# A two-layer graph network: the second layer's frames move from between the layers into the first layer's loop

## What is computed

```
x = layernorm(x + L0(x, edge_index, edge_attr_4, edge_attr_32, ...))
x = layernorm(x + L1(x, edge_weight, edge_attr_3, edge_index, ...))
# L1, per edge:
R = relu(edge_weight[:, None] @ w1 + b1) @ w2 + b2
r = edge_attr_3 / norm(edge_attr_3)
msg = sum over paths of R * (spherical harmonics of r) * x[src] * Wigner 3j
out = out.at[dst].add(msg)
```

## Time and profile before

| | |
|---|---|
| median of 3 runs | 4217.16 us (4216.61 to 4221.31) |
| profiled execution | 4217.1 us, of which the span of its instructions is 4215.3 us |
| busy in the span | PE 3586.2, PEld 2173.2, DVE 3226.0, ACT 2200.7, POOL 3022.9 us |
| layer 0's gathers | first start 27.0, last start 2039.6 us |
| layer 1's gathers | first start 2101.7, last start 4144.9 us |
| granted TensorE clock | 0.934 of full speed in the mean |

### The profile page before, as it was taken

The page is one execution under the profiler, slowest core; times in us unless marked ns, Lnnn a source line. Parts: engine busy times, 40 slices in busy tenths (PEclk is TensorE's granted clock), DMA queues, the critical chain, the costliest instruction groups (busy, mean ns, idle before and its releaser), DMA issues.

```text
span 4215.3 us, 77958 instructions
## 1 busy us (share of the span) xinstructions
PE 3586.2 (85%) x24746; PEld 2173.2 (52%) x24746; DVE 3226.0 (77%) x4478; ACT 2200.7 (52%) x6571; POOL 3022.9 (72%) x3143
## 2 busy tenths in 40 slices
PE   5888888888888888888439999999999999999995
PEld 3555555555555555555315555555555555555553
DVE  6666666666666666666789988888888888888887
ACT  2555555555555555555315555555555555555553
POOL 5777777777777777777357777777777777777772
PEclk7998999999999999999769999999999999999998
DMA  3111111111111111111221221221212122221212
GB/s 101 30 25 30 25 30 30 25 30 25 30 25 30 30 25 30 25 30 25 37 89 39 46 46 37 47 44 39 47 37 47 37 46 44 40 47 37 47 37 32
DMA packets 214486, 159.83 MB, mean 38 GB/s; under 512 B 124769, under 2 KB 188002, under 8 KB 213474
## 3 DMA queue, kind: packets, MB, share of 16 engines
q0 software_dynamic: 100352, 51.58, 8.6%
q1 hardware_dynamic: 84946, 90.16, 8.2%
q10 hardware_dynamic: 29170, 17.88, 1.5%
HBM read 148.94 MB, written 10.43 MB: 38 GB/s over the span
## 4 chain that ended last, share of the span: by engine, by line
POOL 55%; issue 23%; PE 10%; DVE 7%; DMA 3%; DVEq 1%; POOLq 0%; ACT 0%; SPq 0%; ACTq 0%
POOL rows L352 55%; PE red L668 6%; PE wps L655 3%; DVE prod L972 2%; DMA rows<-x_rows,src 2%; DVE q L1024 1%; PE wps L648 1%; DMA src<-in_src 1%; DVE t_a L1010 0%; PE acc L682 0%; DVEq L1052 0%; POOLq L369 0%; DVE table L1048 0%; DVE t_b L896 0%; DVE work L877 0%
## 5 line engine op out<-in xcount | busy, mean ns | idle before, releaser
L352 POOL DMA_INDIRECT rows<-x_rows,src x1568 | 1507.3, 961 | 598.0 <-issue 560.4
L352 POOL DMA_INDIRECT rows<-in_x,src x1568 | 1514.7, 966 | 508.7 <-issue 498.8
L668 PE MATMUL red<-prod,ident 128*128 128x336 f32 (+2 forms) x6272 | 1753.7, 436 | 0.0
L668 PEld LDWEIGHTS red<-prod,ident 128*128 128x128 f32 x6272 | 1145.0, 192 | 647.5 <-issue 189.5
L476 ACT ACTIVATE gap<-iota,slot_plan 128x128 bf16<-128x128 f32 x3136 | 945.7, 387 | 91.9 <-DVE t_b L1075 81.9
L972 DVE TENSOR_TENSOR prod<-wps,q 128x896 f32<-128x896 f32 x784 | 836.6, 1084 | 192.4 <-PE wps L655 175.3
L648 PE MATMUL wps<-bias_parts,ones 64*128 64x448 bf16 (+1 forms) x2352 | 464.1, 391 | 558.9 <-DVE prod L966 330.8
L655 PE MATMUL wps<-w_sb,hidden 64*128 64x256 f32 (+1 forms) x4704 | 910.5, 490 | 0.0
L494 ACT ACTIVATE sums<-red 128x336 f32<-128x336 f32 (+2 forms) x392 | 168.4, 430 | 1074.7 <-PE red L668 1073.7
L648 PEld LDWEIGHTS wps<-bias_parts,ones 64*128 64x128 bf16 x2352 | 114.6, 94 | 1084.7 <-DVE prod L966 430.5
L1006 DVE TENSOR_TENSOR t_a<-rows,geo 128x384 f32<-128x384 f32 x98 | 55.2, 563 | 674.4 <-DMA rows<-in_x,src 674.4
(11 more groups left out here) (123 smaller groups left out, 2993.6 us busy)
## 6 DMA issues: line engine op xcount, KB each, us to landing
mlp<-in_dist SPq DMA_DIRECT2D x196, 256.0 KB
mlp<-in_feat SPq DMA_DIRECT2D x98, 256.0 KB
rows<-in_x,src POOLq DMA_INDIRECT x1568
rows<-x_rows,src POOLq DMA_INDIRECT x1568
frames<-prod ACTq DMA_DIRECT2D x4, 1764.0 KB, 5.8
geo<-frames ACTq DMA_DIRECT2D x98, 72.0 KB
src<-in_src SPq DMA_DIRECT2D x196, 8.0 KB, 1.6
geo<-in_sh ACTq DMA_DIRECT2D x98, 32.0 KB, 1.7
```

Source lines behind the costliest of these rows:

```text
L352: nc.gpsimd.indirect_dma_start(out=rows[z][:, t, :], out_offset=None, in_=table_rows, in_offset=bass.IndirectOffsetOnAxis(ap=src_sb[z][:, ...
L668: ins = nc.tensor.matmul(red[:, bank * 512:bank * 512 + cols], ident[:], pr[:, i, :, a:b, :], start=(i == 0), stop=(i == MUL - 1))
```

## The change

The frames are made two chunks at a time, at the end of body0 of each even chunk (49 times 17 instructions on 32 columns), in a buffer of their own, and ACT stores each piece to the same place in DRAM in the following body. The squares (now on ACT), their sums and the root move to the setup, before the node table. The reciprocal is taken per piece. Before layer 1 only ACT waits, for the count of all stores. ACT's copies of the frames to PSUM in layer 1 are as before, and so is the rest of both loops.

```diff
+        lengths = sb("lengths", [P, CHUNKS * TILES])
+        frame = sb("frame", [P, FRAME_TILES, GEO[1]])
+        frame_tmp = sb("frame_tmp", [P, 5, FRAME_TILES])
...
+            def square_lengths():
+                act.wait_ge(loaded["rel"], 16)
+                for square, ts in zip(squares, square_tiles):
+                    nc.scalar.activation(square, rel_sb[:, ts, :], ACT.Square).then_inc(rel_squared, 1)
+
+            def root_lengths():
+                act.wait_ge(lengths_squared, 2)
+                nc.scalar.activation(lengths[:], lengths[:], ACT.Sqrt).then_inc(lengths_ready, 1)
+
+            def store_frames(i, r):
+                act.wait_ge(frames_ready, r)
+                act.dma_start(frame_dram[:, bass.ds(i * (FRAME_TILES * GEO[1]), FRAME_TILES * GEO[1])],
+                              frame[:].rearrange("p t c -> p (t c)")).then_inc(frames_stored, 16)
...
                         distances(n, z1, r1, 0, steps)
+                    if n == 0 and z == 1:
+                        store_frames(i, r)
                     if not last:
                         load_geo(n, k + RING, z, r + 1)
...
+            square_lengths()
             spread_windows()
+            root_lengths()
             act.wait_ge(loaded["weights"], 64)
...
             deviations(0)
-            store_frames()
-            for b in range(2):
-                act.wait_ge(frames_stored[b], 16 * FRAME_PARTS // 2)
+            act.wait_ge(frames_stored, act.snap(count * (16 * ROUNDS) + 16))
             loop(1, count)
...
+            def measure():
+                for square, ts in zip(squares, square_tiles):
+                    dve.wait_ge(rel_squared, 1 if ts.start == 0 else 2)
+                    nc.vector.tensor_reduce(lengths[:, ts], square, AX_X, ALU.add).then_inc(lengths_squared, 1)
...
             split_bias(1)
+            measure()
             dve.wait_ge(loaded["nodes"], 16)
...
+            def make_frames(i, r, st):
+                u0, u1, u2, a0, a1, a2, b0_, b1_, b2_ = (frame[:, :, c] for c in range(GEO[1]))
+                sign, h, tmp, tmp2, inv = (frame_tmp[:, c, :] for c in range(5))
+                vec = rel_sb[:, bass.ds(i * FRAME_TILES, FRAME_TILES), :]
+                def then(ins):
+                    st.need(st.done(ins))
+                dve.wait_ge(lengths_ready, 1)
+                then(nc.vector.reciprocal(inv, lengths[:, bass.ds(i * FRAME_TILES, FRAME_TILES)]))
+                dve.wait_ge(frames_stored, r * 16)
+                st.done(nc.vector.tensor_tensor(frame[:, :, 0:2], vec[:, :, 1:3],
+                                                inv.unsqueeze(2).broadcast_to([P, FRAME_TILES, 2]), ALU.mult))
+                then(nc.vector.tensor_tensor(u2, vec[:, :, 0], inv, ALU.mult))
+                then(nc.vector.tensor_scalar(sign, u2, 0.0, 2.0, ALU.is_ge, ALU.mult))
+                then(nc.vector.tensor_scalar(sign, sign, -1.0, None, ALU.add))
+                then(nc.vector.tensor_tensor(h, sign, u2, ALU.add))
+                st.done(nc.vector.scalar_tensor_tensor(out=a2, in0=u0, scalar=-1.0, in1=sign, op0=ALU.mult,
+                                                       op1=ALU.mult))
+                then(nc.vector.reciprocal(h, h))
+                st.done(nc.vector.tensor_scalar(b2_, u1, -1.0, None, ALU.mult))
+                st.done(nc.vector.tensor_tensor(tmp, u0, h, ALU.mult))
+                then(nc.vector.tensor_tensor(tmp2, u1, h, ALU.mult))
+                st.done(nc.vector.tensor_tensor(tmp, a2, tmp, ALU.mult))
+                then(nc.vector.scalar_tensor_tensor(out=b0_, in0=u0, scalar=-1.0, in1=tmp2, op0=ALU.mult, op1=ALU.mult))
+                st.done(nc.vector.tensor_tensor(tmp2, u1, tmp2, ALU.mult))
+                st.done(nc.vector.tensor_tensor(a1, sign, b0_, ALU.mult))
+                then(nc.vector.tensor_scalar(a0, tmp, 1.0, None, ALU.add))
+                then(nc.vector.tensor_tensor(b1_, sign, tmp2, ALU.subtract))
+                dve.sem_inc(frames_ready, 1)
...
                 add_window(3, cols, z1, st)
+                if z == 0:
+                    make_frames(i, r, Steps(dve, frame_steps, (r - 1) * FRAME_STEPS))
...
             normalize(0)
-            make_frames()
             first_windows()
             dve.wait_ge(x1_stored, 16)
```

64 lines of the change are left out of this document (12 added, 52 removed).

## The result

The changed kernel takes **4181.9 us** (median; 4180.82 to 4187.6), the kernel before 4216.92 in the same series: ratio 0.9916, 95% interval 0.9904 to 0.9929. So it is 0.8% faster, 35 us. The forecast was 4194 with a range from 4183: right in sign and in where the gain comes from, 12 us too slow, and 1.1 us outside the range. The profiled execution took 4180.8 us, of which 4179.0 are span, 36.3 less than the span of before.

A forecast was written before the change was run, and what follows sets the result against it. The prediction took GpSimd's gathers to bound the kernel, with 36 us idle between the layers. From 4215.3 us, -36.1 there, +10 for held gathers and +2.8 at layer 0's end gave 4192.0 of span, so 4194 us, range 4183 to 4208.

The forecast's parts named there:

- What bounds the kernel: Layer 0's loop and layer 1's are paced by GpSimd's gathers; GpSimd idles 36.1 us between the layers while VectorE makes frames.
- Part 1, the seam: Between the layers: without the frames there, layer 1's fifth chunk starts gathering 36.1 us earlier, about 2184.5; -36.1 us.
- Part 2, the piece's length: Layer 0's loop: 17 VectorE instructions on 32 columns take 4.8 us a round, just fitting about 5.0 us of idle.
- Part 2, the point from which lateness costs: Layer 0's loop: VectorE reading rows late costs nothing until frames exceed some 10.5 us a round, using up both idles.
- Part 3, the holding: Layer 0's loop: frame instructions lengthen GpSimd's gathers through a shared resource, 0.20 us a round, +10 us over 49 rounds.
- Part 4, layer 0's end: After layer 0's last gathers: the last piece delays the message and what follows by +2.8 us, bounds 1.7 and 12.
- Part 5, setup: Setup: squares, sums and root moved there cost nothing, as VectorE makes up its lateness; bounds -1 and +3 us.
- The sum: Whole kernel: 4215.3 - 36.1 + 10 + 2.8 = 4192.0 us of span, so 4194 us; range 4183 to 4208.
- No holding: Rival for layer 0's loop: short pieces slip between the gathers' needs, holding term 0, 4184 us; chance 0.12.
- VectorE late, other phases: Rival for layer 0's loop: frames exceed the idle, later projection work meets other gather starts, 4209 us; chance 0.10.
- The slower one: Rival for layer 0's loop: gathers held as beside the old frames, 1.25 us a round, 4245 us; chance 0.05.

The follow-up runs named there:

- setup part alone: Kernel before with only squares, sums and root of the lengths moved to the setup, other frame work still between the layers: 4205.84 us, ratio 0.9969.
- 5.45 us of piece: Changed kernel with each piece computed on 80 columns instead of 32, the rest thrown away: 4195.73 us, ratio 0.9949.
- 6.2 us of piece: Changed kernel with four unused two-input products on 384 columns behind each piece: 4230.94 us, ratio 1.0028.
- the two slowest kernels: Changed kernel with four unused 384-column products behind each piece, 4230.94 us; changed kernel with the 16 instructions after each piece's first reciprocal made twice, 4231.69 us.

## Why the prediction was right and wrong

- **What bounds the kernel: right.** GpSimd's pace, and its idle of 36 us at the seam. The setup part alone gives back its own time, 11.9 us for 11.7.
- **Part 1, the seam: right.** Forecast -36.1, measured -36.1; that it fits to 0.1 us is luck, since in the six other kernels with the frames out of the seam the fifth chunk starts 83.2 to 83.9 us after the first gather, not 82.9. The x1 store is late next (first gather 12.05 us after the normalization's end, 12.07 before), and 82.9 us to the fifth chunk is what was forecast (2184.5 less 2101.66 is 82.8). The new wait is 2.94 us.
- **Part 2, the piece's length: too long.** 4.8 us forecast, 3.64 measured. The instructions were priced well (two inputs 0.19 to 0.23, one input 0.18 to 0.21, reciprocals 0.35 and 0.34). Of the 1.2 us, 1.0 is the ten waits at 0.13: after a wait on VectorE's own instruction the next starts 0.03 to 0.04 us behind the end of the one before (1029.81 + 0.21 to 1030.06). The 0.13 came by subtraction from one pair of L1048, the wrong pair to price a wait from. That the piece fits its cover is right.
- **Part 2, the point from which lateness costs: wrong,** though it didn't touch this result. "Beyond some 10.5 us a round" should read 4.7 for the phases and 6.4 for VectorE as the bound. Three things failed. The idle without the register loads is 4.7 us a chunk, 9.4 for two, where the prediction had 5.0 and made 10.5 of two; that is the small part. TensorE's chain takes 9.7 us from product to product, so VectorE can't catch up in the odd chunk; no view of before shows it, because in that trace the landing ends the wait. And GpSimd's pace depends on phases, not on buffers alone.
- **Part 3, the holding: the step that failed.** +10 forecast, +0.3 to +0.7 measured in the loop (last gather against the kernels without pieces and with the setup part alone; 1.1 to 1.3 from the third chunk's first gather). The forecast was 2.4 hits a round (3.8 gather starts, 0.63 of them on instructions that hold) at 0.1 us each. Measured are 2.9 needs a round within the piece (144 in all), of which 0.8 are held, by 0.017 us each: 0.68 us in all. "A hit costs half an instruction" is the step that is wrong. Of the 69 needs that fall in an instruction with two inputs, 31 come in its first 0.14 us, and none of these gathers is longer; 38 come in its last 0.06 us, where no more than 0.03 us is lost. The other needs meet instructions with one input, reciprocals or the gaps between instructions, and none of them costs over 0.02 us. The rule was drawn from instructions of 0.52 and 0.85 us, in which the need came 0.32 and 0.40 us after their start. The projection's first product would have shown it in the trace of before: in 9 chunks the gather's need falls in its first 0.160 us, and none of the nine is held. The case that came nearest was therefore the one with 0.12.
- *The Trainium skill* ("SBUF — State Buffer", "Who interferes with whom") infers that tensor_tensor doesn't stall descriptor generation. By that the term was put at 0, which came nearer than mine. But that a tensor_tensor leaves a gather alone is not what the traces show: L1018, a tensor_tensor with both inputs in SBUF, lengthens gathers by 21.5 us in the changed kernel, and where the gather's need comes early the product is longer instead, by 0.05 us in the case above. Whether what is held is the generation of descriptors or another part of the gather no run here tells. The pieces were spared because their instructions are hardly longer than the delay; that fits the counts, and is not shown by a run of its own. And that the section's rule of two inputs in SBUF "agrees with the rows" holds for L904 alone: L897 is a tensor_scalar, with one.
- **Part 4, layer 0's end: right in kind, too large.** +2.8 forecast, +1.4 measured. L1087 starts 23.8 us after the last gather instead of 21.6, 2.2 later where 3.1 was forecast; the 0.43 us wait behind it vanishes, as said. Of the missing 1.4 us, 0.9 are that earlier start (the piece 1.2 shorter, the register loads 2.0 instead of 1.6) and 0.3 a second wait that vanishes (before L1223, 0.34 us).
- **Part 5, setup: nothing forecast, -1.5 measured** by the third chunk's first gather (73.61 to 72.09), of which 0.6 are already there at the first. The bound was -1. In the seven other kernels with the new setup on these chips that chunk starts at 72.2 to 73.2, so all eight are ahead of the 73.61 of before, by 0.4 to 1.5. Part of it may be a gain of the new setup; against a single trace of before that is not shown, and I have not traced its cause.
- **The sum.** 13.0 us of span between 4192.0 and 4179.0: Part 3 with the loop 11.3 (10 against -1.3), Part 4 1.4, setup 1.5, less 1.3 for layer 1 behind its fifth chunk. The range's lower end stood 1 us under the rival without holding and left no room for the other two terms to come out low with it; that made it too narrow.
- **The rivals.** "No holding" (4184) is what happened, though not because the pieces slip between the needs: they meet them and hold them for next to nothing. "VectorE late, other phases" exists, at 5.45 us of piece. The slower one was put on the wrong mechanism: what makes this change a loss is not holding at the old frames' price but VectorE as the bound, 2.6 us of work a round away (at 6.2 us of piece).

## What to carry to other kernels

Work that is moved beside the bounding engine is nearly free while it fits the real idle in front of one wait (here 4.7 us after the register loads), so measure that idle without its own instructions and keep the piece under it; the first excess costs by phases, long before the engine is full. When the pieces contend with another engine, cut them short: here the pieces' instructions of 0.21 us held a GpSimd gather by 0.03 us at most (0.06 in the two slowest kernels), a window addition of 0.22 us by up to 0.13, and a product of 0.56 us by 0.3 in the mean. And before counting on a later idle to catch up, look for a chain through a third engine that takes its time regardless.

## What the hardware showed beyond that

- Who comes first matters, with a delay: the first product of a projection (0.56 us, both inputs in SBUF) held the gather whose need came 0.167 us or more after its start (366 of 366 over five kernels), and didn't where it came 0.166 us or less after it (50 of 50). For the window additions the delay is shorter, 0.1 us.
- Waiting for the own engine's last instruction costs VectorE 0.03 to 0.04 us between short instructions, and 0.16 before L904 in the loop, where it follows a reciprocal and a second semaphore is waited for. Neither is the cause by itself: in the last piece, which is written out behind the loop, the same L904 starts 0.03 us behind the same reciprocal (2055.02 + 0.35 to 2055.40).
- The same program took 4216 to 4224 us on some chips and 6875 to 6974 on others, with a granted clock of 0.93 against 0.77 to 0.78; the clock alone doesn't account for it.
